# Far products moved ahead of the turns in TensorE's step, and the far exponential moved to the step of its products

## What is computed

```python
scores = jnp.einsum('bhid,bhjd->bhij', q, k) * scale + gated_bias
attn = jax.nn.softmax(scores, axis=-1)
out = jnp.einsum('bhij,bhjd->bhid', attn, v)
```

## Time and profile before

| | |
|---|---|
| median of 3 runs | 3314.15 us (3313.4 to 3319.57) |
| the profiled execution | 3317.36 us |
| its span, first to last instruction | 3315.3 us |
| TensorE busy | 3102.9 us, 94% |
| ScalarE busy | 2060.2 us, 62% |
| VectorE busy | 2385.2 us, 72% |
| steps of attention with turns | from about 244 to 2000 us of the span |

### The profile page before, as it was taken

One profiled execution on the slowest core, in us unless ns is written; L12 is line 12 of the kernel. 1 busy time (PEld: TensorE's weight loads), 2 busy tenths in 40 slices (PEclk: granted clock), 3 DMA queues, 4 the chain that ended last, 5 costly groups with the idle time before them and its releaser, 6 DMA issues. The chain is left out here.

```text
span 3315.3 us, 58248 instructions
## 1 busy us (share of the span) xinstructions
PE 3102.9 (94%) x18893; PEld 2035.9 (61%) x18893; DVE 2385.2 (72%) x5688; ACT 2060.2 (62%) x4106; POOL 1522.3 (46%) x1916
## 2 busy tenths in 40 slices
PE   7988999999999999999999997866999999999991
PEld 4644555555555555554555554755888888888881
DVE  6879998989899899998999994865444444444426
ACT  3548999999999999998999993212233223332330
POOL 3554444444444444444444440004666666666651
PEclk9999999999999999999999998977999999999996
DMA  7982323232323242323232324535667666676666
GB/s 251 312 287 41 67 51 67 51 78 51 68 52 66 67 67 54 67 53 72 53 68 53 67 39 145 169 97 184 209 219 226 206 209 209 220 224 211 212 213 209
DMA packets 274613, 436.24 MB, mean 132 GB/s; under 512 B 58539, under 2 KB 202997, under 8 KB 255637
## 3 DMA queue, kind: packets, MB, share of 16 engines
q1 hardware_dynamic: 233108, 370.94, 40.1%
q0 software_dynamic: 30464, 44.94, 6.4%
q10 hardware_dynamic: 10752, 16.78, 1.4%
HBM read 325.60 MB, written 106.42 MB: 130 GB/s over the span
## 5 line engine op out<-in xcount | busy, mean ns | idle before, releaser
L878 DVE CUSTOM_DVE_ANT_0 tot<-sc,gbias 128x1024 f32<-128x1024 f32 x1024 | 1239.7, 1211 | 16.5 <-POOL gbias L739 16.2
L739 POOL TENSOR_SCALAR gbias<-slab_a,gs 128x484 f32<-128x484 f32 x1024 | 687.3, 672 | 869.1 <-DVE negm L878 848.4
L922 ACT ACTIVATE probs<-tot,negm 128x640 f32<-128x640 f32 (+2 forms) x1024 | 768.0, 750 | 41.7 <-DVE negm L878 33.8
L1507 ACT ACTIVATE f_hid<-f_ph,f_w_up 128x256 f32<-128x256 f32 (+1 forms) x584 | 268.6, 460 | 667.8 <-PE f_ph L1466 653.0
L781 PE MATMUL sc<-ks,qs 120*128 120x512 bf16 x2048 | 616.2, 382 | 27.1 <-DVE negm L878 15.5
L890 DVE COPY wt<-pb 128x256 f32<-128x256 f32 (+1 forms) x1024 | 398.0, 389 | 170.7 <-PE pb L802 170.3
L1466 PE MATMUL f_ph<-f_xt,f_w_up 128*128 128x256 f32 (+1 forms) x2336 | 486.2, 366 | 1.4 <-DVE f_xt L1526 1.2
L1478 PE MATMUL f_py<-f_w_down,f_hid 128*128 128x256 f32 x2176 | 481.6, 379 | 0.0
L947 ACT ACTIVATE wt<-pa 128x256 f32<-128x256 f32 (+1 forms) x1024 | 447.8, 437 | 43.8 <-PE pa L793 30.5
L793 PEld LDWEIGHTS pa<-ident,probs 128*128 128x128 f32 x2560 | 330.0, 140 | 228.2 <-issue 99.0
L1466 PEld LDWEIGHTS f_ph<-f_xt,f_w_up 128*128 128x128 f32 x2336 | 422.0, 191 | 56.4 <-issue 2.6
(11 more groups left out here) (203 smaller groups left out, 3171.5 us busy)
## 6 DMA issues: line engine op xcount, KB each, us to landing
f_w_down<-in_w_down SPq DMA_DIRECT2D x73, 1152.0 KB
f_w_up<-in_w_up SPq DMA_DIRECT2D x73, 1028.0 KB
ks<-k_d SPq DMA_DIRECT2D x192, 128.0 KB, 4.9
qs<-q_d SPq DMA_DIRECT2D x384, 64.0 KB
v_d<-vt SPq DMA_DIRECT2D x16, 1024.0 KB, 6.4
vs<-v_d SPq DMA_DIRECT2D x32, 512.0 KB, 7.1
rcb<-rc_d SPq DMA_DIRECT2D x64, 256.0 KB
q_d<-parts SPq DMA_DIRECT2D x32, 384.0 KB, 4.5
```

The source lines that it names most:

```text
L739: pool.tensor_scalar(gbias[x % NG][:, SIDE:SIDE + BAND], slab[:, hh, :], gs[u % 2][:, i, hh:hh + 1], 1.0, ALU.mult, ALU.mult).then_inc(gbi ...
L878: dve.tensor_tensor_reduce(tot[x % 2][:], sc[:, x % 2, :], gbias[x % NG][:, w:w + N], -1.0, 3.0e38, ALU.add, ALU.min, negm[h % 2][:, c:c + ...
L922: act.activation(probs[x % 2][:, 0:hi - lo], tot[x % 2][:, lo:hi], ACT.Exp, bias=negm[h % 2][:, c:c + 1], scale=-1.0).then_inc(near_done, 1)
```

## The change

In TensorE's step, `far` stands directly behind `scores`, ahead of `turn` and `weigh`. In ScalarE's step x, `exp_far` takes the far tile of step x, where it took the one of step x - 1. Number and kind of instructions, tiles, waits and amounts of data are the same.

```diff
@@ TensorE
                 if x + 2 < NX:
                     scores(x + 2)
+                h, t = (x - NR - FAR_AT) // NR, (x - NR - FAR_AT) % NR
+                if 0 <= h < NH:
+                    far(h, t)
                 if 1 <= x <= NX:
                     turn(x - 1)
                 h, m = (x - NR - AV_AT) // NR, (x - NR - AV_AT) % NR
                 for n in range(AV_N):
                     if 0 <= h < NH and AV_STEP[n] == m:
                         weigh(h, n)
-                h, t = (x - NR - FAR_AT) // NR, (x - NR - FAR_AT) % NR
-                if 0 <= h < NH:
-                    far(h, t)
@@ ScalarE
                 if x < NX:
                     exp_near(x)
-                h, t = (x - 1 - NR - FAR_AT) // NR, (x - 1 - NR - FAR_AT) % NR
+                h, t = (x - NR - FAR_AT) // NR, (x - NR - FAR_AT) % NR
                 if 0 <= h < NH:
                     exp_far(h, t)
```

## The result

| | before | after |
|---|---|---|
| median | 3315.9 us (3313.4 to 3319.57, 4 runs) | 3387.61 us (3386.96 to 3388.2, 4 runs) |
| span of the profiled execution | 3315.3 us | 3385.2 us |
| one half (16 steps), sum of the medians of its steps | 27.28 us | 28.51 us |

The ratio is 1.0212, with a 95% interval from 1.02 to 1.0224. The changed kernel is slower by 72 us; forecast were +61 us and 3375 us.

The account below looks back on a forecast made before the run. TensorE's own work, busy 497 of 500 us, was taken as the bound. New stalls of 1.60 us a half against 0.63 gave +0.97, over 62.7 halves +61 us on 3314.15: 3375 us, range 3333 to 3405.

Parts of the forecast that it names:

- The mechanism: TensorE's turn waits for ScalarE's copy behind the far exponential; new stalls 1.60 us a half against 0.63.
- the wait of `far`: Far tile's wait on the last far exponential goes in steps 1 and 3 (0.09, 0.15); step 15's 0.27 kept.
- Rival A: Faster: ScalarE isn't late for the turn, -15 us, or -32 with step 15 too; chance 0.08.
- Rival B: No change: links to and from ScalarE shorter by 0.15 us together, 3314 within 7 us; chance 0.05.
- The largest term: Steps 9-10, copy of the sums on ScalarE's path: 2.31 us against TensorE's 1.81, a stall of 0.50.
- The small stalls: Turn stalls: pairs 1-2, 3-4 0.20 each, 5-6 0.15, 7-8 0.08, 11-12, 13-14 0.10 each; 15-0 keeps 0.27.
- The price of a load behind a wait: Each waiting turn starts 0.14 us after the copy it waited for ends, as in step 10.
- The low end with 0.05: Turn starts 0.05 us after its wait, like a far tile: 0.35 us a half, +22 us.
- The switches: TensorE's new neighbours (scores to far, far to turn, weighing to scores) priced like the old ones: +0.
- The half of 45 us kept for the high end: Weighing to scores might cost 0.09 us more once a pair, 45 us; taken as 0, half kept for the high end.
- The division's stall: Step 15, stall of 0.27 us from VectorE's division: kept, covering pair 15-0's 0.10.
- rival C: Much slower: DMA of the maxima late for step 6's far tile (0.5 us a half, 3406), or costlier weighing-to-scores; chance 0.07.

Follow-up runs that it names:

- `half_after`: Changed kernel with the exponential of far tiles 8 to 15 of each half taken of 256 of 512 columns, the rest zero: 3355.1 us.
- `raw_late`: Changed kernel with ScalarE's copy of the sums behind the copy of the turned blocks instead of ahead of it: 3357.93 us.
- `division_pool`: Both engines with turn ahead of far (against the changed kernel), and the division on GpSimd instead of VectorE, same step 14: 3303.06 us.

## Why the prediction was right

**The mechanism** was right in all the links that cost time. The turn waits for `wt<-pa`, that stands behind the far exponential, and ScalarE idles ahead of the odd steps' far exponential (0.38 us at 1035.95; 0.37 to 0.93 in steps 1 to 13). One step was wrong without a price: the wait of `far` was to go, and is there in steps 2, 4 and 6, in the shadow of the turn's. `half_after` and `raw_late` each took away one link and got back what the sum gave for it. Rival A was wrong for the reason named: busy shares don't limit a loop of latencies; ScalarE is busy 428 of 500 us and TensorE waits for it. Rival B needed links shorter by 0.15 us; they came out 0.02 longer (1.98 us against 1.96).

**The largest term**, steps 9-10 with the copy of the sums, was +0.38 and came as +0.38.

**The small stalls were mis-sized.** Seven pairs without it were forecast at +0.59 together, and came as +0.85. For 11-12 the timeline shows where it is: 1.98 us for the path instead of 1.96, and 0.03 more for the blocks behind a stall, whose first weight load starts 0.03 us ahead of its product there (1037.04), and 0.11 where nothing waits (1035.64). For 1-2 to 5-6 the path has 0.44 + 0.42 + 0.50 + 0.38 + 0.14 = 1.88 (read in step 3) against 1.85, again with the 0.03. Rounding to 0.01 us in five links, for stalls that are differences of 0.1 of two sums of 1.9, was too coarse. At 62.7 halves, 0.01 us in each of seven pairs is 4 us.

**The price of a load behind a wait** was right: 0.14 to 0.15 us in all the turns that wait, as at 1033.28 to 1033.42. The low end with 0.05 has no row that supports it.

**The switches** that no row of before showed cost nothing: scores follow a weighing as soon as far tiles did (a pair in steps 11-12 has 1.00 us from 1037.74 to 1038.74), a far tile follows the scores in 0.44 where turned blocks took 0.43, and the turn follows a far tile that nothing holds up in 0.22, or 0.17 with three small products. The half of 45 us kept for the high end was not needed.

**The division's stall** The earlier trace rows stayed: step 15, 1.48 to 1.46 us. It now ends at the scores, which wait for the maximum behind the division, instead of at the far tile.

**The DMA of rival C** didn't come late: the far tile of step 6 starts 0.50 us behind the scores (0.49 to 0.52 in steps 2 and 4), and the pair 5-6 is as long as the path through ScalarE. The whole list of waits has one for this DMA, of 1.8 us (0.6 before), behind the steps with turns.

**The sum** of the steps is +1.23 us x 62.7 = 77 us, yet 72 were measured. Some 6 us come back outside the regular steps: the profiled execution before lost 7.3 us there, after 1.1. At three places a slab load has to land before GpSimd goes on, and its landing took 5.5, 5.9 and 7.9 us in the one and 5.9, 5.5 and 5.3 in the other. The one of 7.9 us alone cost 5.8. A landing of 5.9 us cost 0.9 before and 0.7 after, so the slower loop covers a little of it. How much of the 6 us is chance stays open, and that they brought the time nearer to the forecast is luck: the stalls were mis-sized by 0.26 us a half, 16 us, and 11 of these show in the median; the kernel before has a spread of 10 us over 12 runs (3311.8 to 3321.7), the changed one 1.2 in four.

## What to carry to other kernels

When two in-order engines take turns on single buffers, write down the path from one engine's instruction through the other and back, and compare it with the first engine's own work between these two points; the busy shares of neither show it. An instruction that comes once in sixteen steps costs its full length each time if it stands on that path, and nothing one place further on. Before moving an instruction on one engine, look at what the other lists (SyncE's too) have in the same step.

## What the runs showed of the hardware

- VectorE's product of two SBUF operands of 128x512 took 0.68 us alone and 1.05 to 1.12 when a GpSimd product that had started 0.09 to 0.16 us before it ran beside it for 0.51 to 0.58 us. GpSimd's took 0.67 either way.
- The same product took 1.28 us on GpSimd (`division_pool`).
- TensorE's first transpose started 0.14 to 0.15 us after the ScalarE instruction that it waited for had ended, a bf16 product 0.05 to 0.06 (0.14 in step 6, where it waits for a DMA too); three transposes behind such a wait took 0.35 to 0.36 us, not 0.33.
- The load of `slab` (968 KB) landed 4.6 to 7.9 us after it was issued, at the same places of kernels that differ little.
